# A fused attention and spiking feed-forward block: two normalisations' moments on ScalarE, and a new order of TensorE's instructions around the key projection

## The chip, the cores and the metric

The kernel runs on one core of one Trainium2 chip. The metric is the time of the whole program on the device in microseconds (us), the median of several runs. A core has five engines with queues of their own, each of which works in order: TensorE (PE in the profile; PEld is its weight loads), VectorE (DVE), ScalarE (ACT), GpSimd (POOL) and SyncE (SP, which here only issues DMAs). They meet through semaphores: an instruction waits until a counter has reached a value, and everything behind it on its engine waits with it.

## The reference, cut to what matters

```python
# x: (8, 512, 256) float32; H = 16 heads of dk = 16
x = x + layernorm(attention(layernorm(x)))
x = x + layernorm(feed_forward(layernorm(x)))

def attention(x):
    q, k, v = split(x @ W_qkv.T)              # 16 heads
    k = (k - mean(k)) / sqrt(var(k) + 1e-5)   # over the 16 features of a head
    def step(F, t):                           # over 512 tokens
        F = retention * F + coef * outer(v_t, k_t)
        return F, (W_LTM + F) @ q_t
    return scan(step) @ W_o.T

def feed_forward(x):
    y = square(relu(x @ W_fc.T)) @ W_proj.T   # 256 -> 1024 -> 256
    # 5 steps of a spiking neuron driven by y; the mean of its 5 spikes
    return spikes(y) / 5
```

## The kernel before

A batch is 512 tokens, in four tiles of 128 partitions (TILES). The eight batches go through a software pipeline. Iteration g works on up to four of them at once: the recurrence of batch g ("now"), the output projection and the first half of the feed-forward of batch g-1 ("before", b1), the second half and the spikes of batch g-2 ("two_before", b2), and the input normalisation and first projections of batch g+1 ("after", b). An iteration has 16 slots, and each engine's program is a list of calls under `if s == ...`, so that the order on each engine is written out by hand. Iterations 2 to 6 have all four parts; iteration 1 has no b2, iteration 7 has no batch after.

**The recurrence.** In each slot VectorE does two products (`hebbian`, L953) and two scans over the tokens (`scan`, L963). GpSimd multiplies the states by the queries (`read`, L1237, one instruction a slot), and in every second slot TensorE sums eight such products into PSUM (`sums`, L359). A `read` of slot s waits for the scans of s and, since `prod` has four buffers, for `sums` number s // 2 - 1: `read(g, 14)` waits for `sums(g, 5)`, which is in slot 14 of TensorE. `sums(g, 7)`, in slot 1 of the next iteration, waits for `read(g, 15)`. On GpSimd `add_feed_forward` (L1248) stands between `read(g, 14)` and `read(g, 15)`.

**One bank for many.** The PSUM bank p_a holds in turn the projections of value, key and query (`project`, L311), the variance of the keys (`key_variance`, L332), their spread scales (`key_scale`, L341), the transposed x (`turn_x`, L305) and the transposed x1 (`turn_x1`, L399). Each must have been copied out before the next is written. VectorE's `norm_k` (L945) multiplies the keys by p_a after `key_scale`; for half 0 this is the entry to the recurrence of the next batch. The two banks p_c take the output projection (`project_out`, L372), `down` (L381), `count_spikes` (L389) and `up` (L411) by turns.

**Feed-forward.** `up(b1, 0)` to `up(b1, 7)` stand in slots 10 to 15 of TensorE, and `hidden` on ScalarE follows each: relu out of the bank (L684) and square into `ht` (L686). `hidden(b2, 6)` and `hidden(b2, 7)` are in slot 0 of the next iteration, ahead of `square_k(g, 1)` (L641, L642) in slot 1 and of `copy_y(b1, 1)` in slot 2. `project_out(b1, .)` waits for this last copy (`y_done`). `copy_y` and all the other plain copies have the line of one helper, L628.

**Normalisations.** Norms 1 and 4 get their sums and squares from ScalarE with an accumulator (L600, L609; L715, L726). Norms 2 (of the output projection, `oo`) and 3 (of x1) get theirs from VectorE: four bn_stats (L913) and four bn_aggr (L920), then a square root on ScalarE (`deviation`), a reciprocal on VectorE (`scales`, L926) and four scalings on ScalarE (L617). `low_x` and `low_x1` on GpSimd (L1253) make the low parts that the projections and `up` wait for.

Of the kernel before, what the change touches and what calls it, by code (L numbers as in the profile page):

```python
# [16 lines left out]
P = 128  # L17
KT = D // P
# [50 lines left out]
def build(nc, x, w_qkv, w_o, w_fc, w_proj, w_ltm, head_params, shared_params, ident, head_mask, pick, out):  # L69
    ctx = ExitStack()  # L70
    with ctx:
# [6 lines left out]
        def sem(name):  # L78
# [35 lines left out]
        squares = {n: sb(f"squares{n}", [P, TILES]) for n in (1, 4)}  # L114
# [6 lines left out]
        minus_mean = {n: sb(f"minus_mean{n}", [P, TILES]) for n in (1, 4)}  # L121
# [48 lines left out]
            o_proj o_done n2_stats n2_var n2_dev n2_step n2_done x1_done  # L170
            n3_stats n3_var n3_dev n3_step n3_done  x1_turned x1t_done x1t_high x1t_low
# [124 lines left out]
        def _(pe):  # L296
# [18 lines left out]
            def project_v(b, half):  # L315
                pe.wait_ge(S["xt_low"], at(KT * (b + 1)))
                pe.wait_ge(S["k_done"], at(2 * b + half))
                if half == 0: pe.wait_ge(S["x1t_done"], at(KT * (b - 1)))
                project(b, 2 * D + half * P, "v_proj")
# [65 lines left out]
            def count_spikes(b, pair):  # L385
                pe.wait_ge(S["sign_done"], at(2 * b + pair + 1))
                pe.wait_ge(S["yf_done"], at(TILES * b + 3 + pair))
                for j in range(STEPS):
                    last = pe.matmul(p_c[(pair + 1) % 2][:, :], ident_b[:, :], sign[:, pair, j, :, :],  # L389
                                     start=(j == 0), stop=(j == STEPS - 1))  # L390
                last.then_inc(S["count_done"], 1)

            def turn_x1(b, t):
# [3 lines left out]
                pe.wait_ge(S["x1t_done"], at(KT * b + t))  # L397
                for u in range(TILES):
                    last = pe.transpose(p_a[:, tokens(u)], oo[:, u, t * P:(t + 1) * P], ident_sb[:, :])  # L399
# [65 lines left out]
            def iteration(g, now, before, two_before, after):  # L465
                b, b1, b2 = g + 1, g - 1, g - 2
                for s in range(SLOTS):
# [13 lines left out]
                    if now:  # L481
                        if s == 0: project_v(g, 1)
                        if s == 1: project_k(g, 1)
                        if s == 2: key_variance(g, 1)
# [4 lines left out]
                    if now and s == 5: key_scale(g, 1)  # L489
                    if after and s == 6: turn_x(b, 0)  # L490
                    if two_before and 3 <= s < 7: down(b2, s - 3, before)
                    if after:
                        if s == 7: turn_x(b, 1)
                        if s == 10: project_v(b, 0)
                        if s == 11: project_k(b, 0)
                        if s == 13: project_q(b, 0)
                        if s == 14: key_scale(b, 0)
# [5 lines left out]
                    if after and not before and s == 11: key_variance(b, 0)  # L503
                    if before and after:
                        if s == 10: up(b1, 0)
                        if s == 11:
                            up(b1, 1)
                            key_variance(b, 0)
                            up(b1, 2)
                        if s == 13:  # L510
                            up(b1, 3)
                            up(b1, 4)
                        if s == 14: up(b1, 5)
                        if s == 15:
                            up(b1, 6)
                            up(b1, 7)
# [60 lines left out]
        def _(act):  # L577
# [9 lines left out]
            def deviation(n, b):  # L587
                act.wait_ge(S[f"n{n}_var"], at(b + 1))
                if n in (1, 4):
                    eps = eps_sb[:, 0:1] if n == 1 else eps_sb[:, 2:3] if b == LAST - 1 else eps_sb[:, 1:2]  # L590
                    nc.scalar.activation(dev[n - 1][:, :], squares[n][:, :], ACT.Sqrt, bias=eps, scale=1.0 / D).then_inc(
                        S[f"n{n}_dev"], 1)
                else:
                    nc.scalar.activation(dev[n - 1][:, :], moments[n - 1][:, :, 1], ACT.Sqrt, bias=eps_sb[:, 0:1]).then_inc(
                        S[f"n{n}_dev"], 1)

            def total_x(b):
# [5 lines left out]
                nc.scalar.activation(minus_mean[1][:, :], total[1][:, :], ACT.Identity, scale=-1.0 / D).then_inc(  # L603
                    S["n1_mean"], 1)

            def squares_x(b):
                act.wait_ge(S["n1_mean"], b)
                for u in range(TILES):
                    last = nc.scalar.activation(passed[:, u, :], xa[:, u, :], ACT.Square, bias=minus_mean[1][:, u:u + 1],  # L609
# [65 lines left out]

            def copy_x1t(b, t):
                act.wait_ge(S["x1t_low"], at(KT * (b - 1) + t + 1))
                copy(p_a[:, :], x1f[:, t, :], "x1_turned", KT * b + t + 1, "x1t_done")
# [17 lines left out]
            def signs(b, pair):  # L696
                act.wait_ge(S["yf_done"], at(TILES * b + 2 * (pair + 1)))
                act.wait_ge(S["count_done"], at(2 * (b - 1) + pair + 1))
                for j in range(STEPS):
                    last = nc.scalar.activation(sign[:, pair, j, :, :], yf[:, 2 * pair:2 * pair + 2, :], ACT.Sign,  # L700
                                                bias=drive_sb[:, j:j + 1], scale=BELOW_ONE)
                last.then_inc(S["sign_done"], 1)
# [35 lines left out]
            nc.scalar.activation(dev[0][:, :], moments[0][:, :, 1], ACT.Sqrt, bias=eps_sb[:, 0:1]).then_inc(S["n1_dev"], 1)  # L738
            norm1(0)
# [20 lines left out]
            def iteration(g, now, before, two_before, after):  # L760
                b, b1, b2 = g + 1, g - 1, g - 2
                for s in range(SLOTS):
# [6 lines left out]
                    if s == 0:  # L769
                        if after: total_x(b)  # L770
                        if now: copy_v(g, 1)
                        if two_before:
                            hidden(b2, 6)
                            hidden(b2, 7)
                    if s == 1:
                        if now: square_k(g, 1)
                    if s == 2:
# [5 lines left out]
                    if s == 3:  # L783
# [3 lines left out]
                        if now: copy_q(g, 1)  # L787
                        if after: norm1(b)
                    if s == 4:
                        if before: deviation(2, b1)  # L790
                        if now: spread_k(g, 1)
# [8 lines left out]
                    if s == 7:  # L800
                        if now: copy_key(g)
                        if before: deviation(3, b1)
# [5 lines left out]
                    if s == 9:  # L808
# [5 lines left out]
                        if two_before: signs(b2, 1)  # L814
                        if two_before and after: squares_count(b2, 0)
                    if s == 10:
                        if after: copy_v(b, 0)
                        if two_before and after:
                            total_count(b2, 1)
# [4 lines left out]
                    if s == 11:  # L824
                        if now: copy_y(g, 0)
                        if after: square_k(b, 0)
                        if two_before and after: deviation(4, b2)
                        if before and after: hidden(b1, 0)
                        if after: key_deviation(b, 0)
                        if before and after: hidden(b1, 1)  # L830
# [555 lines left out]
```

## Time and profile before

| | |
|---|---|
| median of 3 runs | 573.79 us (570.6, 573.79, 579.51) |
| the profiled execution: its time, its span | 574.97 us, 573.2 us |
| busy share of the span: PE, PEld, DVE, ACT, POOL | 83%, 55%, 94%, 60%, 67% |
| mean granted clock of TensorE | 0.926 of full speed |
| busy time of VectorE's two large groups, L963 and L953 | 308.8 us and 170.9 us |

The span runs from the first to the last instruction; 1.8 us of the execution's time lie around it. Busy shares are means over stages with different limits, and an engine can be idle for a wait that costs nothing. For a pipeline such as this one the useful question is which chain of waits closes on itself in one iteration.

### The profile page before, as it was taken

The page shows a single profiled execution, that of the slowest core. Times are in us where ns is not written, and L with a number is a line of the kernel's source. Part 1 is how long each engine was busy: PE and PEld are TensorE (multiplying, and loading weights), DVE is VectorE, ACT ScalarE, POOL GpSimd, SP SyncE. Part 2 cuts the span into 40 slices and gives each one's busy share as a digit, 9 for nine tenths or more (in the row PEclk, how much of TensorE's full clock was granted, in tenths as well). Part 3 has the DMA queues.
Part 4 walks back from the last instruction along what each step waited for, and adds up shares of the span by engine and source line. Part 5 has one row for each costly group of instructions (what it writes and reads, how often), then busy time and mean ns, then how long its engine had stood idle before and what let it go on. Part 6 is the DMA issues. An engine that isn't in the chain of part 4 may idle for free.

```text
span 573.2 us, 7812 instructions
## 1 busy us (share of the span) xinstructions
PE 474.5 (83%) x2245; PEld 313.6 (55%) x2252; DVE 539.0 (94%) x858; ACT 341.3 (60%) x788; POOL 386.7 (67%) x206
## 2 busy tenths in 40 slices
PE   4683567549989899979998899989997999897992
PEld 2451234225677466736675557756673667565881
DVE  5699999999999999999999999999999999997767
ACT  5461343444565986687767886697758745763331
POOL 1138996587857968696968794897769686783022
PEclk9698687858989899999999998989999999999997
DMA  7475577556573568647685649455942778410002
GB/s 263 138 196 145 145 186 199 138 154 162 136 206 107 144 168 239 179 116 202 175 211 150 172 122 245 122 152 125 288 135 94 183 215 221 134 39 8 29 2 73
DMA packets 54778, 87.64 MB, mean 153 GB/s; under 512 B 5456, under 2 KB 19408, under 8 KB 54736
## 3 DMA queue, kind: packets, MB, share of 16 engines
q1 hardware_dynamic: 54160, 87.12, 56.2%
q8 instruction: 18, 0.29, 0.2%
q14 instruction: 24, 0.20, 0.1%
q10 hardware_dynamic: 576, 0.03, 0.1%
HBM read 78.74 MB, written 8.39 MB: 152 GB/s over the span
## 4 chain that ended last, share of the span: by engine, by line
PE 54%; DVE 18%; issue 12%; POOL 8%; ACT 6%; DMA 1%; SPq 0%; DVEq 0%; POOLq 0%; ACTq 0%
PE p_c L381 13%; PE p_c L411 11%; DVE state L963 9%; PE p_a L311 7%; PE p_y L359 6%; POOL prod L1237 5%; PE p_c L372 4%; PE p_a L332 2%; PE p_y L350 2%; DVE p_u L953 2%; PE p_a L305 2%; POOL x1t L1253 2%; PE p_u L550 1%; DVE yf L1189 1%; PE p_a L341 1%
## 5 line engine op out<-in xcount | busy, mean ns | idle before, releaser
L1237 POOL TENSOR_TENSOR prod<-state,qf 128x1024 f32<-128x1024 f32 x127 | 300.8, 2375 | 120.3 <-DVE state L963 60.2
L963 DVE TENSOR_TENSOR_SCAN state<-ret,p_u 128x512 f32<-128x512 f32 x256 | 308.8, 1207 | 0.0
L953 DVE TENSOR_TENSOR p_u<-vrep,p_k 128x512 f32<-128x512 f32 x256 | 170.9, 673 | 0.1
L381 PE MATMUL p_c<-wproj_sb,ht 128*128 128x256 f32 x448 | 102.0, 381 | 0.0
L381 PEld LDWEIGHTS p_c<-wproj_sb,ht 128*128 128x128 f32 x448 | 83.5, 190 | 16.8 <-issue 5.0
L311 PE MATMUL p_a<-xt,wqkv_s 128*128 128x512 f32 x276 | 85.1, 448 | 5.7 <-POOL xt L1253 2.1
L411 PE MATMUL p_c<-x1t,wfc_s 128*128 128x512 f32 x324 | 82.7, 401 | 2.3 <-ACT hr L684 1.0
L359 PE MATMUL p_y<-prod,summer 128*32 128x512 f32 x512 | 75.5, 664 | 7.9 <-POOL prod L1237 6.5
L311 PEld LDWEIGHTS p_a<-xt,wqkv_s 128*128 128x128 f32 x276 | 55.2, 210 | 46.0 <-issue 18.7
L411 PEld LDWEIGHTS p_c<-x1t,wfc_s 128*128 128x128 f32 x324 | 59.5, 188 | 18.9 <-POOL x1t L1253 3.4
L700 ACT ACTIVATE sign<-yf,drive_sb 128x512 bf16<-128x512 f32 x60 | 38.1, 710 | 0.2
L684 ACT ACTIVATE hr<-p_c 128x512 f32<-128x512 f32 x56 | 33.2, 593 | 6.5 <-PE p_c L411 5.2
L686 ACT ACTIVATE ht<-hr 128x512 f32<-128x512 f32 x56 | 35.4, 632 | 1.8
L359 PEld LDWEIGHTS p_y<-prod,summer 128*32 128x32 f32 x512 | 10.4, 111 | 37.2 <-issue 25.0
L628 ACT COPY vf<-p_a 128x512 f32<-128x512 f32 x15 | 8.7, 577 | 34.3 <-PE p_a L311 34.3
L372 PE MATMUL p_c<-wo_sb,yt 128*128 128x256 f32 x112 | 28.9, 416 | 0.0
L332 PE MATMUL p_a<-mean_sb,ksq 128*128 128x8 f32 x128 | 17.7, 265 | 13.1 <-ACT ksq L642 13.1
L332 PEld LDWEIGHTS p_a<-mean_sb,ksq 128*128 128x128 f32 x128 | 16.6, 203 | 19.3 <-ACT ksq L642 19.3
L305 PE MATMUL p_a<-ident_sb,xa 128*128 128x128 f32 x64 | 11.9, 317 | 15.8 <-issue 8.0
L372 PEld LDWEIGHTS p_c<-wo_sb,yt 128*128 128x128 f32 x112 | 23.0, 211 | 3.4
L1253 POOL TENSOR_TENSOR xt<-xf,xt 128x512 fp32r<-128x512 f32 x16 | 20.7, 1291 | 5.9 <-ACT xt L628 5.7
L305 PEld LDWEIGHTS p_a<-ident_sb,xa 128*128 128x128 f32 x64 | 8.3, 160 | 25.8 <-issue 14.1
(188 smaller groups left out, 596.4 us busy)
## 6 DMA issues: line engine op xcount, KB each, us to landing
vrep<-v_rows SPq DMA_DIRECT2D x256, 256.0 KB, 4.4
xa<-in_x SPq DMA_DIRECT2D x9, 512.0 KB, 5.0
v_rows<-vf SPq DMA_DIRECT2D x16, 256.0 KB, 2.9
x<-in_x SPq DMA_DIRECT2D x7, 512.0 KB, 6.9
out<-x SPq DMA_DIRECT2D x7, 512.0 KB, 3.3
ht<-in_w_fc SPq DMA_DIRECT2D x1, 1024.0 KB, 7.3
wproj_sb<-in_w_proj SPq DMA_DIRECT2D x1, 1024.0 KB, 10.2
state<-in_w_qkv SPq DMA_DIRECT2D x1, 512.0 KB, 5.9
```

Of the source, the lines that this page charges most:

```text
L311: last = pe.matmul(bank[:, :], wqkv_s[:, i, t, first_col:first_col + P], xt[:, j, t, :], start=(t == i == j == 0), stop=(t == KT - 1 and i ...
L332: last = pe.matmul(p_a[:, u * HH:(u + 1) * HH], ksq[:, u * P:(u + 1) * P], mean_sb[:, :], start=True, stop=True)
L359: last = pe.matmul(p_y[32 * grp:32 * grp + 32, :], summer[:, half, dl, grp, :], prod[:, s % NZ, grp % 2, :], start=False, stop=(dl == 3), ...
L372: last = pe.matmul(p_c[(t + 1) % 2][:, i * D:(i + 1) * D], yt[:, half, tokens(2 * t + i)], wo_sb[:, half, :], start=(half == 0), stop=(hal ...
L381: last = pe.matmul(p_c[(u + 1) % 2][:, 0:D], ht[:, f, tokens(u)], wproj_sb[:, f, :], start=(f == 0), stop=(f == FT - 1))
L411: last = pe.matmul(p_c[(f + 1) % 2][:, :], wfc_s[:, i, t, f * P:(f + 1) * P], x1t[:, j, t, :], start=(t == i == j == 0), stop=(t == KT - 1 ...
L684: nc.scalar.activation(hr[:, f % 2, :], p_c[(f + 1) % 2][:, :], ACT.Relu).then_inc(S["relu_done"], 1)
L686: nc.scalar.activation(ht[:, f, :], hr[:, f % 2, :], ACT.Square).then_inc(S["h_done"], 1)
L700: last = nc.scalar.activation(sign[:, pair, j, :, :], yf[:, 2 * pair:2 * pair + 2, :], ACT.Sign, bias=drive_sb[:, j:j + 1], scale=BELOW_ONE)
L953: v.tensor_tensor(p_u[n % NU][:, :], vrep[:, n % NV, :], p_k[:, :], ALU.mult).then_inc(S["hebb_done"], 1)
L963: v.tensor_tensor_scan(state[:, s % NS, i, :], ret[:, r:r + 1].broadcast_to([P, L]), p_u[n % NU][:, :], 0.0, ALU.mult, ALU.add).then_inc(S ...
L1237: p.tensor_tensor(prod[:, s % NZ, :, :], state[:, s % NS, :, :], qf[:, s // HS, :].unsqueeze(1).broadcast_to([P, 2, L]), ALU.mult).then_in ...
```

## The change

- Norms 2 and 3 lose `statistics` and `moments_of` on VectorE. `squares_o(b1)` in slot 3 of ScalarE squares the four tiles of `oo` with an accumulator (its mean is zero, since W_o is centred), and `squares_x1(b1)` in slot 7 squares the four tiles of x1 with the mean of x as bias. That mean now has to live for three batches, so `minus_mean[1]` becomes three buffers `minus_mean_x`.
- `up(., 7)` goes from slot 15 of TensorE to slot 1 of the next iteration, between `project_k(g, 1)` and `key_variance(g, 1)`; `hidden(b2, 7)` goes behind `square_k(g, 1)`.
- The second half of `turn_x1` goes to the bank p_c[0] and no longer waits for the copy of the first. `count_spikes` of pair 1 then waits for that copy.
- `project_k(b, 0)` follows `project_v(b, 0)` at once in slot 10. For this the five `signs(b2, 1)` on ScalarE are split: two, then `copy_v(b, 0)`, then three, `square_k(b, 0)`, and only then the squares and totals of the counts.
- `key_variance(b, 0)` goes ahead of `up(b1, 1)`, and `key_scale(b, 0)` from slot 14, behind `sums(g, 5)`, to slot 13, ahead of it. `key_scale(g, 1)` goes from slot 5 to slot 4, ahead of a `down`. On ScalarE `norm1(b)` goes behind `spread_k(g, 1)`.

```diff
@@ TensorE
             def project_v(b, half):
-                if half == 0: pe.wait_ge(S["x1t_done"], at(KT * (b - 1)))
+                if half == 0: pe.wait_ge(S["x1t_done"], at(KT * (b - 1) - 1))
...
             def count_spikes(b, pair):
+                if pair == 1: pe.wait_ge(S["x1t_done"], KT * (b + 2))
...
             def turn_x1(b, t):
-                pe.wait_ge(S["x1t_done"], at(KT * b + t))
+                pe.wait_ge(S["x1t_done"], at(KT * (b - 1) + t + 1))
+                if t == 1: pe.wait_ge(S["yf_done"], at(TILES * b))
+                bank = p_a if t == 0 else p_c[0]
...
                         if s == 1: project_k(g, 1)
+                        if s == 1 and two_before: up(b2, 7)
                         if s == 2: key_variance(g, 1)
...
-                    if now and s == 5: key_scale(g, 1)
                     if after and s == 6: turn_x(b, 0)
+                    if now and s == 4: key_scale(g, 1)
...
-                        if s == 10: project_v(b, 0)
-                        if s == 11: project_k(b, 0)
+                        if s == 10:
+                            project_v(b, 0)
+                            project_k(b, 0)
                         if s == 13: project_q(b, 0)
-                        if s == 14: key_scale(b, 0)
...
                         if s == 11:
+                            key_variance(b, 0)
                             up(b1, 1)
-                            key_variance(b, 0)
                             up(b1, 2)
                         if s == 13:
                             up(b1, 3)
                             up(b1, 4)
+                            key_scale(b, 0)
                         if s == 14: up(b1, 5)
-                        if s == 15:
-                            up(b1, 6)
-                            up(b1, 7)
+                        if s == 15: up(b1, 6)
@@ ScalarE
+            def squares_o(b):
+                act.wait_ge(S["o_done"], 2 * (b + 1))
+                for u in range(TILES):
+                    last = nc.scalar.activation(passed[:, u, :], oo[:, u, :], ACT.Square,
+                                                accum_out=squares[2][:, u:u + 1])
+                last.then_inc(S["n2_var"], 1)
+
+            def squares_x1(b):
+                act.wait_ge(S["n1_mean"], b + 1)
+                act.wait_ge(S["x1_done"], b + 1)
+                for u in range(TILES):
+                    last = nc.scalar.activation(passed[:, u, :], x1[b % 2][:, u, :], ACT.Square,
+                                                bias=minus_mean_x[b % 3][:, u:u + 1], accum_out=squares[3][:, u:u + 1])
+                last.then_inc(S["n3_var"], 1)
...
                     if s == 0:
                         if now: copy_v(g, 1)
-                        if two_before:
-                            hidden(b2, 6)
-                            hidden(b2, 7)
+                        if two_before: hidden(b2, 6)
                     if s == 1:
                         if now: square_k(g, 1)
+                        if two_before: hidden(b2, 7)
...
                         if now: copy_q(g, 1)
+                        if before:
+                            squares_o(b1)
+                            deviation(2, b1)
+                    if s == 4:
+                        if now: spread_k(g, 1)
                         if after: norm1(b)
-                    if s == 4:
-                        if before: deviation(2, b1)
-                        if now: spread_k(g, 1)
...
                         if now: copy_key(g)
-                        if before: deviation(3, b1)
+                        if before:
+                            squares_x1(b1)
+                            deviation(3, b1)
...
-                        if two_before: signs(b2, 1)
-                        if two_before and after: squares_count(b2, 0)
+                        if two_before and after: signs(b2, 1, 0, 2)
+                        if two_before and not after: signs(b2, 1)
                     if s == 10:
                         if after: copy_v(b, 0)
+                        if two_before and after: signs(b2, 1, 2, 3)
+                        if after: square_k(b, 0)
                         if two_before and after:
+                            squares_count(b2, 0)
                             total_count(b2, 1)
                             squares_count(b2, 1)
...
                         if now: copy_y(g, 0)
-                        if after: square_k(b, 0)
                         if two_before and after: deviation(4, b2)
-                        if before and after: hidden(b1, 0)
                         if after: key_deviation(b, 0)
-                        if before and after: hidden(b1, 1)
+                        if before and after:
+                            hidden(b1, 0)
+                            hidden(b1, 1)
@@ VectorE
-                    if before and s == 4:
-                        statistics(2, b1, oo, "o_done", 2 * (b1 + 1))
-                        moments_of(2, b1)
...
-                    if before and s == 7:
-                        statistics(3, b1, x1[b1 % 2], "x1_done", b1 + 1)
-                        moments_of(3, b1)
```

## Rows read from the trace of the kernel before

**Rows 1.** The page, parts 1 and 4: busy time, and the chain that ended last.
```profile
PE 474.5 (83%) x2245; PEld 313.6 (55%) x2252; DVE 539.0 (94%) x858; ACT 341.3 (60%) x788; POOL 386.7 (67%) x206
...
PE 54%; DVE 18%; issue 12%; POOL 8%; ACT 6%; DMA 1%; SPq 0%; DVEq 0%; POOLq 0%; ACTq 0%
```

**Rows 2.** Timeline of VectorE, start, duration, [idle before]: norm_k at an iteration's end.
```profile
88.72 0.67 DVE L945 TENSOR_TENSOR p_k<-p_a,kc 128x512 f32<-128x512 f32 x1
...
149.41 0.70 DVE L945 TENSOR_TENSOR p_k<-p_a,kc 128x512 f32<-128x512 f32 x1 [0.69 <-PE p_a L341]
...
211.73 0.70 DVE L945 TENSOR_TENSOR p_k<-p_a,kc 128x512 f32<-128x512 f32 x1 [0.88 <-PE p_a L341]
...
272.73 0.70 DVE L945 TENSOR_TENSOR p_k<-p_a,kc 128x512 f32<-128x512 f32 x1 [0.68 <-PE p_a L341]
...
457.03 0.70 DVE L945 TENSOR_TENSOR p_k<-p_a,kc 128x512 f32<-128x512 f32 x1 [0.68 <-PE p_a L341]
```

**Rows 3.** Who TensorE waited for, iteration 4 (272.7 to 333.7): us, times, longest.
```profile
PE p_c L389 <- ACT sign L700: 1.8, 1, 1.8
PE p_a L332 <- ACT ksq L642: 1.4, 1, 1.4
PE p_a L399 <- ACT oo L617: 1.1, 1, 1.1
PE p_a L399 <- ACT x1f L628: 0.9, 1, 0.9
```

**Rows 4.** Timeline of VectorE in iteration 4: the moments of norm 3.
```profile
303.57 1.38 DVE L913 BATCH_NORM_STATS2 stats<-x 128x6 f32<-128x256 f32 x4
304.98 0.38 DVE L920 BATCH_NORM_AGGREGATE moments<-stats 128x2 f32<-128x6 f32 x4
```

**Rows 5.** Groups by line: one square with an accumulator over 128x256.
```profile
L609 ACT ACTIVATE passed<-xa,minus_mean 128x256 f32<-128x256 f32 x28 | 13.8, 496 | 0.0
```

**Rows 6.** Timeline of GpSimd in slot 9 of iteration 4: the last low part of x.
```profile
312.94 1.28 POOL L1253 TENSOR_TENSOR xt<-xf,xt 128x512 fp32r<-128x512 f32 x1
```

**Rows 7.** Timeline of TensorE: project_k(b, 0) right behind project_v(b, 0), in iteration 0.
```profile
72.00 2.93 PE L311 MATMUL p_a<-xt,wqkv_s 128*128 128x512 f32 x6 [0.73 <-ACT vf L628]
```

**Rows 8.** Timeline of ScalarE in slot 11 of iteration 4: the copy in square_k(b, 0).
```profile
322.18 0.59 ACT L641 COPY kc<-p_a 128x512 f32<-128x512 f32 x1 [0.41 <-PE p_a L311]
```

**Rows 9.** Timeline of TensorE from the end of iteration 3 into iteration 4.
```profile
271.05 1.07 PE L359 MATMUL p_y<-prod,summer 128*32 128x512 f32 x8
272.04 0.66 PE L341 MATMUL p_a<-ident_sb,krx 128*128 128x128 f32 x4
272.45 4.45 PE L411 MATMUL p_c<-x1t,wfc_s 128*128 128x512 f32 x18
...
279.46 1.06 PE L359 MATMUL p_y<-prod,summer 128*32 128x512 f32 x8
...
284.43 3.70 PE L372 MATMUL p_c<-wo_sb,yt 128*128 128x256 f32 x16
```

**Rows 10.** Timeline of GpSimd in the same stretch: read 14, add_feed_forward, reads 15 and 0.
```profile
272.29 2.41 POOL L1237 TENSOR_TENSOR prod<-state,qf 128x1024 f32<-128x1024 f32 x1 [0.48 <-PE p_y L359]
274.66 2.40 POOL L1248 TENSOR_TENSOR x<-x,spk 128x1024 f32<-128x1024 f32 x1
277.02 4.75 POOL L1237 TENSOR_TENSOR prod<-state,qf 128x1024 f32<-128x1024 f32 x2
```

**Rows 11.** Timeline of ScalarE in the same stretch: hidden(b2, 7), then copy_y.
```profile
281.24 0.58 ACT L684 ACTIVATE hr<-p_c 128x512 f32<-128x512 f32 x1
281.86 0.63 ACT L686 ACTIVATE ht<-hr 128x512 f32<-128x512 f32 x1
...
283.35 0.59 ACT L628 COPY yt<-p_y 128x512 f32<-128x512 f32 x1
```

**Rows 12.** project_out's matmuls in two stretches of iteration 2: us, PE busy, PEld busy, PEclk, DMA share, GB/s.
```profile
160.90:164.30 3.40, 3.03 (x7) 2.56 (x8) 0.50 1.05 268
161.20:166.50 5.30, 5.21 (x16) 4.09 (x16) 0.70 1.05 263
```

## What the change should do to the time

> **What bounds the kernel now.** I read the page first: VectorE is busy 94% of the span, yet the chain that ended last runs 54% on TensorE and 18% on VectorE [rows 1]. So the fullest engine isn't plainly the limit. The timeline of VectorE settles the size of an iteration by `norm_k`, its last step: 60.7 us for iteration 1 (88.72 to 149.41), 62.3 us for iteration 2, 61.0 us for iteration 3, and 307.6 us for iterations 2 to 6 together (149.41 to 457.03), that is three of 61.0 and two of 62.3 [rows 2]. At each of these entries but the first VectorE stands idle for 0.7 to 0.9 us until TensorE's `key_scale` is there [rows 2]. VectorE is thus nearly full, but it is TensorE that lets it in.
>
> The next view is who TensorE waited for: in iteration 4 it waits four times, 1.8, 1.4, 1.1 and 0.9 us, 5.2 us in all, always for ScalarE and never for VectorE [rows 3]. TensorE's own loop, about 55.8 us of work and 5.2 us of round trips, makes the 61.0 us. The change takes work from VectorE and goes for three of those four waits. What counts is whether the loop of TensorE gets shorter.
>
> **VectorE's part.** Four bn_stats and four bn_aggr take 303.57 to 305.28, 1.7 us [rows 4]; norms 2 and 3 have a set each, so 3.4 us leave VectorE in each of iterations 1 to 7. Where TensorE sets the pace these 3.4 us become idle time in front of `norm_k` or of a reciprocal. Where VectorE does, they come off the time. ScalarE gets twice 4 x 0.496 = 2.0 us [rows 5]. In slot 7 these come in place of a wait for the moments, which ended at 305.36 [rows 4]: from the copies ahead of it on ScalarE I work out 305.3 for the new squares too, so nothing is gained or lost on x's way to its low part and on to `project_v(b, 0)`. Bounds for each set: 0 and its own 2.0 us late.
>
> **Two banks.** `turn_x1(., 1)` waits 0.9 us for the copy of the first half [rows 3], and no longer will. But `project_v(b, 0)` also needs the last low part of x, which GpSimd makes from 312.94 to 314.22 [rows 6], just when TensorE comes by today. The chain to it (`sums(g, 1)`, three reads, two low parts) doesn't change. I take 0; the other end is 0.9 us an iteration. The Trainium skill ("Perfetto Trace Analysis", Optimizing Tensor Performance, Matmuls) advises rotating independent matmul groups through different banks, so that one is copied out under the next. By that rule the 0.9 us would be won; the low part's row speaks against it here.
>
> **Key projection at once, variance one tile ahead.** Behind `project_v` TensorE will wait 0.7 us for the copy of the values, as in iteration 0 [rows 7], in place of the 1.8 us for the signs [rows 3]. But `up(b1, 2)` still needs ScalarE's first relu, and ScalarE has the same list to do before it, only in another order. It loses one idle 0.41 us [rows 8], gains 0.2 us of waiting for the end of `project_v`, and the second bank has spared it 0.2. I take 0.3 us earlier for `project_q(b, 0)`; bounds 0 and 1.1 (1.8 - 0.7). `key_scale(b, 0)` ahead of `sums(g, 5)` then costs its 0.4 us (272.04 to 272.45 [rows 9]) on the way to `sums(g, 5)`, which so comes 0.1 us later than today.
>
> **The last up tile.** It is moved into the 1.4 us in which TensorE waits for the squares of the keys before `key_variance(g, 1)` [rows 3]. What it leaves behind is the question. Today `sums(g, 5)` starts at 271.05 and `sums(g, 7)` at 279.46 [rows 9]. Between them GpSimd does read 14 (which waits for `sums(g, 5)`), add_feed_forward and read 15: 272.29 to 279.4, with no gap [rows 10]. So `sums(g, 7)` starts the moment read 15 is done, and TensorE is there at that moment too, because it had `key_scale`, three up tiles, `sums(g, 6)` and `project_v` to do. Take out `key_scale` (0.4) and one up tile (1.45, a third of the 4.4 us of the three in L411's row [rows 9]) and TensorE is there 1.8 us early and waits. The 1.4 us filled are given back in front of `sums(g, 7)`. Gain 0.
>
> And there is a new wait. `hidden(b2, 7)` now stands ahead of `copy_y(b1, 1)` on ScalarE and cannot start before `up(b2, 7)` is done; behind `copy_y` stands TensorE's `project_out(b1, 0)`. From the start of `sums(g, 7)` to `project_out` it is 279.46 to 284.43, 4.97 us [rows 9]. After: the sums 1.0, `project_k` 1.5 (six matmuls of 512 columns like an up tile), the up tile 1.5 and about 0.15 to the end of its last matmul, 0.1 to ScalarE, relu and square until the next instruction starts 1.17 (0.62 + 0.55), `copy_y` 0.59, 0.05 back to TensorE [rows 9, 11]: 6.06 us (I put the two hand-overs at 0.1 and 0.05 as an estimate). That is 1.1 us more in each iteration with b2. TensorE would wait about 1 us at L372.
>
> **The sum.** The period of iterations 2 to 6: 61.0 + 0.1 + 1.1 = 62.2 us, five times +1.2 = +6.0. Iteration 1 has no b2, so neither `up(b2, 7)`, hidden(b2, 7) nor add_feed_forward. TensorE is idle there while VectorE sets the pace: of the 3.4 us I take 2.9, since a wait of ScalarE's new squares for x1 gives some back (bounds 2 and 3.4). Iteration 7 again waits for TensorE at the start, and later VectorE must wait at norm 3 for x1: 0.3 gained, bounds 0 and 3.4. Iteration 0 and the tail: 0. Sum: +6.0 - 2.9 - 0.3 = +2.8 us.
>
> **The clock.** Iteration 2, of 62.3 us, has its `project_out` in 5.21 instead of 3.70 us [rows 9, 12], at a granted clock of 0.50 of full speed (1.2 GHz) in the stretch after 160.90; just before it TensorE waits for the squares of the keys and does the small matmuls of the variance, as it does in every iteration [rows 3]. Only iteration 2's is in the rows; I put the second iteration of 62.3 us down to the same, and keep these 2 x 1.3 us as they are: TensorE's idle time in an iteration goes from 5.2 to about 6.5 us, but is spread out.
>
> So 573.2 + 2.8 = 576.0 us of span, and 577.8 for that execution with its 1.8 us around the span. The median shown is 1.2 us under the profiled execution: 576.6 us.
>
> **Rivals.**
> *Faster, VectorE is the bound.* If the 3.4 us come off every iteration from 1 to 7, 24 us go: 550 us. For it: the 94%. Against it: the 0.7 us at each `norm_k`, which then would have to go as well. It holds if TensorE's loop falls to 57.6 us, so all four waits must go. Chance 0.05. The Trainium skill ("Perfetto Trace Analysis", Identifying the Most-Contended Engine) would have one look at the engine with the highest occupancy, here VectorE, and shorten it first, with this result.
> *Faster, the waits simply go.* If GpSimd's read 15 is done when TensorE comes to `sums(g, 7)`, the 1.4 us are kept, and the change of order at the value projection gives 1.0: a period of 58.6 us, 5 x 2.4 = 12 us, with the 3 us of iterations 1 and 7 and the 2.6 us of slow clock also gone: 556 us. It decides at read 15: it would have to end 1.8 us sooner, for which read 14 would have to start before `sums(g, 5)` ends. Chance 0.11.
> *Same, only one of my two waits.* Without the wait of `project_out`: 5.5 us less than my sum, 571 us. Or with the wait at `project_out` but the up tile's gain kept: 570 us. Chance 0.24.
> *Slower by the clock.* More short waits next to short matmuls could bring the lower clock in every iteration, behind the variance and behind the transposes. A slow `project_out` costs 1.5 us, a slow projection behind the transposes about as much by the same doubling of six matmuls' 1.4 us: 3.0 us in five iterations instead of the 2.6 now is +12.4: 589 us. From two further slow stretches an iteration on it decides. Chance 0.10. The Trainium skill ("TensorE: Matmul & The Clock Gate", A second HAM failure mode) tells of frequent micro-idles between matmul groups that make the clock swing between its two levels; by that the whole loop would be in this case.
> *My sum:* chance 0.50, with 572 to 582 us as its own range.
>
> **Numbers.** The range of 8 in 10 leaves out the two faster rivals (0.16) and the far end of the slower one: 563 to 587 us. A change of under 2% (11.5 us) is about what a measurement of this kernel can't tell from none. Faster by more, under 562.3 us: 0.16. Slower by more, over 585.3: 0.10. Within: 0.74.
>
> **What would show it.** In the profile after: VectorE's busy time down by 24 us to about 515, and its waits for the reciprocals (L926) and `norm_k` up by as much. A wait of TensorE at L359 for GpSimd's prod of 1.8 us in each of iterations 3 to 6; one at L372 for ScalarE's yt of 1 us; one at the second L311 of slot 10 for vf of 0.7 us; none at L332. `norm_k` to `norm_k` 62.2 us. If L359 shows no such wait and the period is under 60, the sum is wrong at read 15. If L372 doesn't wait, it is wrong at `copy_y`. If VectorE has no more idle time than now, the first rival is right.

## The result, and the profile after

| | before | after |
|---|---|---|
| median of 20 runs | 574.22 us | 577.12 us |
| the profiled execution: its time, its span | 574.97 us, 573.2 us | 580.05 us, 578.2 us |
| busy share: PE, PEld, DVE, ACT, POOL | 83, 55, 94, 60, 67% | 83, 55, 89, 63, 67% |
| mean granted clock of TensorE | 0.926 | 0.921 |

The ratio is 1.0046, with a 95% interval of 1.0024 to 1.0068: a little slower, and under 2%. The forecast median was 576.6 us. The profiled execution of the changed kernel took 2.9 us more than the median, so an average execution may have fewer of the slow stretches that its trace shows below. VectorE has 24.5 us less to do [rows 1] and the kernel gains nothing by it. The page after, busy time:

```profile
PE 478.6 (83%) x2245; PEld 319.3 (55%) x2252; DVE 514.5 (89%) x746; ACT 365.2 (63%) x901; POOL 385.6 (67%) x206
```

The timeline of VectorE after, `norm_k` for half 0 (L969 now; start, duration), for rows 2:

```profile
87.04 0.67 DVE L969 TENSOR_TENSOR p_k<-p_a,kc 128x512 f32<-128x512 f32 x1
...
144.50 0.67 DVE L969 TENSOR_TENSOR p_k<-p_a,kc 128x512 f32<-128x512 f32 x1
...
205.00 0.68 DVE L969 TENSOR_TENSOR p_k<-p_a,kc 128x512 f32<-128x512 f32 x1
...
270.05 0.68 DVE L969 TENSOR_TENSOR p_k<-p_a,kc 128x512 f32<-128x512 f32 x1
...
335.11 0.67 DVE L969 TENSOR_TENSOR p_k<-p_a,kc 128x512 f32<-128x512 f32 x1
...
396.93 0.67 DVE L969 TENSOR_TENSOR p_k<-p_a,kc 128x512 f32<-128x512 f32 x1
...
458.77 0.67 DVE L969 TENSOR_TENSOR p_k<-p_a,kc 128x512 f32<-128x512 f32 x1
```

Iteration 1 now takes 57.5 us (60.7 before). Iterations 2 to 6 take 60.5, 65.1, 65.1, 61.8 and 61.8, together 314.3 us against 307.6 [rows 2]. Iteration 0 is 1.7 us shorter, and from the last of these lines to the end it is 119.4 us against 116.2. The sum, -1.7 - 3.2 + 6.7 + 3.2, is the 5.0 us between the two spans.

Who TensorE waited for after, in iteration 5 (333 to 395 us; us in total, times, longest), for rows 3. The lines are `sums` (L360), `turn_x1` (L403), `project_out` (L373), `project` (L312) and `up` (L415):

```profile
PE p_y L360 <- POOL prod L1255: 1.8, 1, 1.8
PE p_a L403 <- ACT oo L618: 1.1, 1, 1.1
PE p_c L373 <- ACT yt L629: 1.1, 1, 1.1
PE p_a L312 <- POOL xt L1271: 0.9, 1, 0.9
PE p_a L312 <- ACT vf L629: 0.7, 1, 0.7
PE p_c L415 <- ACT hr L700: 0.5, 1, 0.5
```

Two more, of 0.2 us each, are left out. Of the four waits of before one is still there (L403, 1.1 us). The three that went, 4.1 us, have become five that come to 5.0. Two of these decide, and the timelines of TensorE, ScalarE and GpSimd after show them at the start of iteration 5 (`norm_k` at 335.11), for rows 9, 11 and 10:

```profile
338.67 1.06 PE L360 MATMUL p_y<-prod,summer 128*32 128x512 f32 x8
339.67 1.66 PE L312 MATMUL p_a<-xt,wqkv_s 128*128 128x512 f32 x6
343.10 1.07 PE L360 MATMUL p_y<-prod,summer 128*32 128x512 f32 x8 [1.77 <-POOL prod L1255]
344.10 1.66 PE L312 MATMUL p_a<-xt,wqkv_s 128*128 128x512 f32 x6
345.59 1.54 PE L415 MATMUL p_c<-x1t,wfc_s 128*128 128x512 f32 x6
346.97 1.02 PE L333 MATMUL p_a<-mean_sb,ksq 128*128 128x8 f32 x8
349.05 3.69 PE L373 MATMUL p_c<-wo_sb,yt 128*128 128x256 f32 x16 [1.05 <-ACT yt L629]
```

```profile
347.17 0.60 ACT L700 ACTIVATE hr<-p_c 128x512 f32<-128x512 f32 x1 [0.29 <-PE p_c L415]
347.80 0.63 ACT L702 ACTIVATE ht<-hr 128x512 f32<-128x512 f32 x1
348.33 0.57 ACT L629 COPY yt<-p_y 128x512 f32<-128x512 f32 x1
```

```profile
335.96 2.43 POOL L1255 TENSOR_TENSOR prod<-state,qf 128x1024 f32<-128x1024 f32 x1 [0.84 <-PE p_y L360]
338.32 2.41 POOL L1266 TENSOR_TENSOR x<-x,spk 128x1024 f32<-128x1024 f32 x1
340.67 4.71 POOL L1255 TENSOR_TENSOR prod<-state,qf 128x1024 f32<-128x1024 f32 x2
```

`key_variance` (L333) follows the moved up tile without a gap, so the wait it was moved into is gone. But TensorE stands for 1.77 us in front of `sums(g, 7)` until read 15 is done (the first of the two in GpSimd's last line, half of 4.71 us, so at about 343.0), and for 1.05 us more in front of `project_out`, because ScalarE takes relu and square of this very up tile before it copies `yt`.

And where VectorE's time went, its longest waits after, over the whole span (us, times, longest):

```profile
DVE rdev L950 <- ACT dev L595: 39.2, 13, 4.8
...
DVE p_k L969 <- PE p_a L342: 1.0, 1, 1.0
```

It now stands in front of the reciprocals, for ScalarE's square roots. Before, it waited at `norm_k` (5.5 us in seven waits over the whole span).

### The profile page after: what moved, and what is told of

Same layout as the page of the kernel before. It is cut to its first block, busy times and chain, and to the rows that moved or that the text cites. A ratio compares the mean times of both kernels' runs of the same rounds, so it can differ in the third digit from the quotient of the medians.

```text
span 578.2 us, 7797 instructions
## 1 busy us (share of the span) xinstructions
PE 478.6 (83%) x2245; PEld 319.3 (55%) x2252; DVE 514.5 (89%) x746; ACT 365.2 (63%) x901; POOL 385.6 (67%) x206
## 4 chain that ended last, share of the span: by engine, by line
PE 54%; DVE 17%; issue 10%; POOL 9%; ACT 8%; DMA 1%; SPq 0%; DVEq 0%; POOLq 0%; ACTq 0%
PE p_c L382 15%; DVE state L987 11%; PE p_c L415 10%; PE p_y L360 8%; PE p_a L312 7%; POOL prod L1255 6%; PE p_c L373 5%; DVE p_u L977 2%; PE p_y L351 2%; ACT sign L716 2%; PE p_a L306 2%; POOL xt L1271 2%; ACT passed L742 1%; PE p_u L555 1%; PE p_a L342 1%
## 5 line engine op out<-in xcount | busy, mean ns | idle before, releaser
L382 PE MATMUL p_c<-wproj_sb,ht 128*128 128x256 f32 x448 | 100.4, 379 | 0.0
L312 PE MATMUL p_a<-xt,wqkv_s 128*128 128x512 f32 x276 | 83.5, 441 | 11.9 <-POOL xt L1271 6.3
L415 PE MATMUL p_c<-x1t,wfc_s 128*128 128x512 f32 x324 | 84.3, 404 | 4.4 <-ACT hr L700 3.6
L360 PE MATMUL p_y<-prod,summer 128*32 128x512 f32 x512 | 73.1, 645 | 17.2 <-POOL prod L1255 15.7
L312 PEld LDWEIGHTS p_a<-xt,wqkv_s 128*128 128x128 f32 x276 | 52.8, 202 | 51.9 <-issue 17.8
L415 PEld LDWEIGHTS p_c<-x1t,wfc_s 128*128 128x128 f32 x324 | 60.3, 191 | 25.9 <-issue 11.9
L950 DVE RECIPROCAL rdev<-dev 128x4 f32<-128x4 f32 x29 | 4.8, 166 | 39.6 <-ACT dev L595 39.2
L373 PE MATMUL p_c<-wo_sb,yt 128*128 128x256 f32 x112 | 34.3, 475 | 6.5 <-ACT yt L629 6.5
L360 PEld LDWEIGHTS p_y<-prod,summer 128*32 128x32 f32 x512 | 10.4, 111 | 46.9 <-issue 26.0
L373 PEld LDWEIGHTS p_c<-wo_sb,yt 128*128 128x128 f32 x112 | 26.6, 242 | 11.9 <-issue 6.8
L642 ACT COPY kc<-p_a 128x512 f32<-128x512 f32 x16 | 9.3, 583 | 30.5 <-PE p_a L312 30.5
L629 ACT COPY yf<-p_c 128x256 f32<-128x256 f32 x28 | 10.1, 361 | 28.1 <-PE p_c L382 28.1
L629 ACT COPY qf<-p_a 128x512 f32<-128x512 f32 x15 | 8.8, 586 | 23.9 <-PE p_a L312 23.9
```

The lines of the kernel that those rows point to most:

```text
L312: last = pe.matmul(bank[:, :], wqkv_s[:, i, t, first_col:first_col + P], xt[:, j, t, :], start=(t == i == j == 0), stop=(t == KT - 1 and i ...
L360: last = pe.matmul(p_y[32 * grp:32 * grp + 32, :], summer[:, half, dl, grp, :], prod[:, s % NZ, grp % 2, :], start=False, stop=(dl == 3), ...
L373: last = pe.matmul(p_c[(t + 1) % 2][:, i * D:(i + 1) * D], yt[:, half, tokens(2 * t + i)], wo_sb[:, half, :], start=(half == 0), stop=(hal ...
L382: last = pe.matmul(p_c[(u + 1) % 2][:, 0:D], ht[:, f, tokens(u)], wproj_sb[:, f, :], start=(f == 0), stop=(f == FT - 1))
L415: last = pe.matmul(p_c[(f + 1) % 2][:, :], wfc_s[:, i, t, f * P:(f + 1) * P], x1t[:, j, t, :], start=(t == i == j == 0), stop=(t == KT - 1 ...
```

## The experiments

The ratio is that of each kernel's runs to the runs of the kernel before on the same chip. The period is `norm_k` to `norm_k` in iterations 3 to 6 at full clock, from the trace. The median of the kernel before was 573.6 to 575.3 us from one set of runs to the other, so a difference between medians of two sets is uncertain by 1 to 2 us, and the ratios are the better measure there.

| | median | ratio to before (95%) | period |
|---|---|---|---|
| the change | 577.1 us | 1.0046 (1.0024 to 1.0068) | 61.8 us |
| copy_y first | 563.8 us | 0.981 (0.978 to 0.984) | 60.6 us |
| up 7 back | 567.1 us | 0.987 (0.984 to 0.990) | 60.6 us |
| read 15 first | 568.2 us | 0.987 (0.982 to 0.991) | 61.6 us, never at full clock |
| both edits | 553.8 us | 0.963 (0.961 to 0.966) | 58.8 us |
| both, low part earlier | 554.9 us | 0.966 (0.964 to 0.969) | 58.3 us |
| both, moments on VectorE | 568.2 us | 0.990 (0.988 to 0.992) | 60.1 us |
| moments alone, on before | 572.9 us | 0.998 (0.996 to 1.000) | 60.6 us |
| two banks alone, on before | 576.0 us | 1.003 (1.001 to 1.006) | 61.0 us |
| read 15 first, on before | 575.1 us | 1.001 (0.998 to 1.004) | 61.0 us |
| the change, wait filled | 571.1 us | 0.996 (0.992 to 0.999) | 61.8 us |

### copy_y first: the wait at project_out

```diff
                     if s == 1:
                         if now: square_k(g, 1)
-                        if two_before: hidden(b2, 7)
                     if s == 2:
                         if before: copy_y(b1, 1)
+                        if two_before: hidden(b2, 7)
```

> The changed kernel with copy_y(b1, 1) back ahead of hidden(b2, 7) on ScalarE; nothing else. My theory: TensorE's wait for yt in front of project_out (1.1 us in each of iterations 2 to 7) is on the loop, so about 6 us go: 571 us, norm_k to norm_k 60.7 us in an iteration at full clock. Rival: the wait only takes up slack that GpSimd or VectorE would take otherwise: 577 us and 61.8 us as in the changed kernel.

Two lines exchanged, and 13.4 us less than with the change. The timeline of TensorE of this run, the same place in the iteration:

```profile
330.03 1.07 PE L360 MATMUL p_y<-prod,summer 128*32 128x512 f32 x8 [1.78 <-POOL prod L1255]
...
333.90 1.02 PE L333 MATMUL p_a<-mean_sb,ksq 128*128 128x8 f32 x8
334.78 3.70 PE L373 MATMUL p_c<-wo_sb,yt 128*128 128x256 f32 x16
```

`project_out` now follows the variance at once. The wait in front of the sums is as long as ever. The period falls by 1.2 us, as expected; the 7 us that this makes in six iterations are half of what was measured. The other half is put down to the clock: no iteration from 2 to 6 of this trace is slower than 60.65 us, and the granted clock is 1.00 in each, where the changed kernel has two iterations of 65.1 and four with a `project_out` of 5.38 us (iterations 2, 3, 4 and 7). The mechanism was right and the size was half of the truth.

### up 7 back: what the move of the tile is worth

```diff
-                        if s == 1 and two_before: up(b2, 7)
...
-                        if s == 15: up(b1, 6)
+                        if s == 15:
+                            up(b1, 6)
+                            up(b1, 7)
```

with `hidden(b2, 7)` back in slot 0 of ScalarE.

> The changed kernel with up(., 7) back in slot 15 and hidden(., 7) back in slot 0. My theory: sums(g, 7) starts when read 15 ends either way. The wait of 1.8 us at the sums shrinks to about 0.3, the wait of 1.2 us for the squares of the keys is back, and the wait for yt is gone: 571 us, like the run with copy_y first. Rival, that filling the wait in front of key_variance is worth its 1.4 us and only copy_y's place spoils it: undoing both gives 1.1 back and loses 1.4 in five iterations, 578 to 579 us.

The waits of TensorE in its iteration 5 (330 to 392 us):

```profile
PE p_a L333 <- ACT ksq L644: 1.2, 1, 1.2
...
PE p_y L360 <- POOL prod L1256: 0.4, 1, 0.4
```

The 1.2 us for the squares of the keys are back, and those for read 15 are down from 1.8 to 0.4. The period is 60.6 us, the same as with the tile moved and `copy_y` first. So moving the tile gains nothing as long as read 15 holds the sums: it only says where TensorE waits. Iteration 2 is the check: there no add_feed_forward stands ahead of read 15 and TensorE doesn't wait at L360 in either run, and with the tile moved (copy_y first) it takes 57.6 us, with the tile back 59.2, both at full clock. So the fill is worth 1.6 us where read 15 doesn't hold the sums. This run measured 3.4 us longer than copy_y first; besides iteration 2, its trace has two iterations of 62.3 us, with a stretch at the lower clock.

### read 15 first, and both edits

```diff
                     if s == 0 and before: read(b1, SLOTS - 1)
+                    if s == 0 and before and g >= 3: add_feed_forward(g - 3)
...
-                    if two_before and after and s == 15: add_feed_forward(b2)
```

and `store_out`, which waits for the result, in slot 3 and no longer in slot 2.

> The changed kernel with add_feed_forward moved on GpSimd from ahead of read 15 to behind it (slot 0 of the next iteration), and the store that waits for it one slot later. My theory: sums(g, 7) waits 1.8 us for read 15 only because of these 2.4 us; without them the wait goes and the loop is 1.8 us shorter in iterations 3 to 7: 568 us, period 60.0 us. Rival: something else holds the loop (VectorE, ScalarE): 577 us.

The median is as expected, 568.2 us, but the period is not. The wait at L360 is gone, and the 1.1 us at L373 are left. Here is `project_out` in this run, and the stretch in which it ran (us, then busy time of PE, PEld, DVE, ACT, POOL with counts, the granted clock, DMA share, GB/s):

```profile
340.05 5.38 PE L373 MATMUL p_c<-wo_sb,yt 128*128 128x256 f32 x16 [1.05 <-ACT yt L629]
```

```profile
339.90:343.30 3.40, 3.25 (x8) 2.66 (x9) 3.30 (x6) 2.45 (x11) 3.06 (x2) 0.56 1.06 283
```

5.38 us and not 3.7, at a granted clock of 0.56 on the mean of the stretch: behind the wait the clock was at the lower level, 1.2 GHz, and in this trace so in each of iterations 2 to 6, at the same place. 61.6 less these 1.7 us is the 60.0 us expected.

> The changed kernel with both edits: copy_y first and read 15 ahead of add_feed_forward. My theory: the two add up, period 61.8 - 1.1 - 1.8 = 58.9 us, 15 us less: 562 us. VectorE's own work, about 57.5 us an iteration, is not reached yet. Rival: each hides behind the other or a third wait (the squares of the keys, ScalarE's relu) takes their place: 568 us.

Both edits together give 553.8 us and a period of 58.8 us, against 58.9 expected. The whole is 8 us shorter than expected. The clock accounts for it: in this trace no iteration from 2 to 6 takes over 58.8 us, and the granted clock is 1.00 in each. Its row on the page, 40 slices of the span in tenths of full speed:

```profile
PEclk9786558958999999999999999999999999999997
```

And the timeline of TensorE, with neither wait:

```profile
323.60 1.66 PE L312 MATMUL p_a<-xt,wqkv_s 128*128 128x512 f32 x6
325.19 1.07 PE L360 MATMUL p_y<-prod,summer 128*32 128x512 f32 x8
326.19 1.65 PE L312 MATMUL p_a<-xt,wqkv_s 128*128 128x512 f32 x6
327.68 1.54 PE L415 MATMUL p_c<-x1t,wfc_s 128*128 128x512 f32 x6
329.06 1.02 PE L333 MATMUL p_a<-mean_sb,ksq 128*128 128x8 f32 x8
329.94 3.70 PE L373 MATMUL p_c<-wo_sb,yt 128*128 128x256 f32 x16
```

This is the best version: 3.7% less than the kernel before, 4.0% less than the changed one by their medians.

### The parts of the change alone

**Moments alone**: the kernel before, with only the moments of norms 2 and 3 moved to ScalarE, in their old slots.

> The kernel before with one part of the change: the moments of norms 2 and 3 by ScalarE, in the same slots. My theory: the loop of iterations 2 to 6 stays at 61.0 us, VectorE is idle 3.4 us more in each, and only iteration 1 gets about 3 us shorter: 571 us. Rival, that VectorE at 94% is the bound: 3.4 us in each of seven iterations, 550 us.

572.9 us. The period goes from 61.0 to 60.6 us, so 0.4 us an iteration were to be had, not 0 and not 3.4. VectorE, with 3.4 us less to do, is busy 57.10 us of 60.60 in iteration 5 and waits for the rest, 1.0 us of it in front of `norm_k` at full clock (0.7 before; 1.67 in the first line, at the end of an iteration of 62.1 us) and 1.5 us in front of a reciprocal, where it did not wait before. Its timeline in this run:

```profile
331.18 0.70 DVE L963 TENSOR_TENSOR p_k<-p_a,kc 128x512 f32<-128x512 f32 x1 [1.67 <-PE p_a L342]
...
364.06 0.18 DVE L944 RECIPROCAL rdev<-dev 128x4 f32<-128x4 f32 x1 [1.50 <-ACT dev L591]
```

The first rival, that VectorE sets the pace at 94%, falls with this run. ScalarE's new squares don't hide a gain either: TensorE's four waits of rows 3 are there with the same lengths to 0.1 us. Iteration 1 became 1.9 us shorter, where about 3 were expected.

**Two banks alone**: the kernel before, with only the second half of `turn_x1` in p_c[0].

> The kernel before with one part of the change: the second half of turn_x1 in its own bank. My theory: the wait of 0.9 us in front of the second transposes goes and comes back in front of project_v(b, 0), which needs the last low part of x from GpSimd: 574 us, no change. Rival, the rule that such a rotation wins the wait: 0.9 us in six iterations, 569 us.

576.0 us, a little slower rather than faster, and the period stays at 61.0 us. From the waits of TensorE around iteration 5 of this run:

```profile
PE p_a L311 <- POOL xt L1256: 1.1, 1, 1.1
```

The 0.9 us for the copy [rows 3] are gone and stand again, as 1.1 us, in front of `project_v`, which waits for the low part of x. The small loss isn't settled: in this trace iterations 1, 2, 4 and 6 have a stretch at the lower level (iteration 1 takes 63.4 us), in that of the kernel before iterations 1, 2 and 5.

**Read 15 first, on the kernel before.**

> The kernel before with read 15 ahead of add_feed_forward, and nothing of the change. My theory: in the kernel before TensorE comes to the sums just when read 15 is done, so ending it 2.4 us earlier is worth at most some tenths: 574 us, period 61.0 us. Rival: read 15 holds the loop already before the change: 1 to 2 us in five iterations, 565 to 569 us.

575.1 us, period 61.0 us. The same edit that takes 9 us from the changed kernel takes nothing from the one before. Read 15 becomes a wait only once the up tile and `key_scale` have left the stretch in front of the sums.

### With both edits: the next limits

> The run with both edits, but with the moments of norms 2 and 3 back on VectorE. My theory: with TensorE's loop at 58.9 us, VectorE's 57.5 + 3.4 = 60.9 us become the bound: 571 to 573 us. Rival: VectorE still has slack, and the time stays at that of both edits, 562 us.

568.2 us, 14.4 more than with the moments on ScalarE. In the changed order the 3.4 us on VectorE do count: in iteration 4 of this run VectorE is busy 59.93 of 60.00 us and waits for nobody. (`deviation(2, b1)` stays in slot 3 of ScalarE and there waits for VectorE's moments, but no wait comes back to VectorE from it.) The moments are worth 0.4 us an iteration in the kernel before, and 1.3 us once TensorE's loop is shorter than VectorE's work. It is somewhat faster than expected: 60.1 us where I had put 60.9, from a floor of 57.5 that was 0.7 too high. In both edits alone VectorE is busy 56.99 of 59.0 us:

```profile
330.00:389.00 59.00, 55.58 (x285) 37.66 (x285) 56.99 (x73) 49.01 (x127) 47.73 (x24) 1.00 0.66 179
```

> The run with both edits, and the last low part of x one slot earlier on GpSimd, ahead of read 8. My theory: the wait of 0.9 us in front of project_v(b, 0) goes, and with two banks nothing else stands there; up(b1, 2) still needs the first relu, so 0.5 to 0.9 us in five iterations: 3 us less than both edits alone, 559 us. VectorE's floor of 57.5 us comes near. Rival: ScalarE's list up to the first relu is the bound there: no change to both edits alone.

```diff
-                    if after and s in (7, 9): low_x(b, (s - 7) // 2)
+                    if after and s in (7, 8): low_x(b, s - 7)
```

The wait for the low part goes, and the next wait of TensorE, for `vf`, grows from 0.7 to 1.3 us: ScalarE is not done with the transposes and the first two signs. The period is 58.3 us, 0.4 less, of the 0.5 to 0.9 expected. The median is no lower. In the profiled execution of this run iteration 0 took 61.9 us instead of 59.3, for a reason told below, which hides a gain of this size. The edit moves the low part in iteration 0 too, so that this loss may be its own.

### The clock: the wait filled

```diff
                 pe.wait_ge(S["relu_done"], at(FT * b - 1 + t))
+                if b >= 1 and t == 0:
+                    for i in range(2):
+                        pe.matmul(p_c[1][:, 0:D], wo_sb[:, 0, 0:P], wo_sb[:, 0, :], start=True, stop=True)
                 pe.wait_ge(S["y_done"], at(2 * (b + 1)))
```

> The changed kernel with two extra matmuls (0.84 us together at full clock, their output is overwritten) in TensorE's wait for yt in front of project_out. The wait itself, its place and the order on ScalarE stay. My theory: the granted clock falls behind this wait because TensorE does next to nothing there but the eight small matmuls of the variance; with work in it the clock stays up, the period stays at 61.8 us and the two iterations of 65 us go: 570 to 572 us. Rival: it is the wait of 1.8 us in front of the sums, two stages earlier, that brings the clock down: 577 us as in the changed kernel.

571.1 us, by work that nobody needs (the two matmuls are four instructions in the trace): 6.0 us less than the change by the medians, 5.2 by the ratios. The period stays at 61.8 us:

```profile
335.44 1.06 PE L360 MATMUL p_y<-prod,summer 128*32 128x512 f32 x8 [1.77 <-POOL prod L1258]
...
340.18 1.11 PE L372 MATMUL p_c<-wo_sb 128*128 128x256 f32 x4
341.28 3.72 PE L376 MATMUL p_c<-wo_sb,yt 128*128 128x256 f32 x16
```

`project_out` starts where it did, but at full clock, in 3.72 us in every iteration from 2 to 7. One iteration of 63.3 us is left, whose slow stretch comes right behind the wait for the sums. So the lower clock can come behind that wait as well; in this trace it does so once.

## Why the prediction was right, point by point

**The bound.** That TensorE's loop sets the pace and VectorE only fills it is shown by moments alone (0.4 us an iteration of the 3.4) and by VectorE's 39.2 us in front of the reciprocals.

**Two banks: 0.** Shown by two banks alone. After the change the wait is there as predicted, 0.9 us at L312 for `xt`.

**The up tile: 0, for read 15.** The wait is 1.8 us as worked out, in iterations 3 to 6. In iteration 2 it isn't there, and the 0 was wrong: the sum has its +1.2 for five iterations, though the wait was named for 3 to 6 only. Shown from both sides: the tile back gives the same period as `copy_y` first, and the wait goes when read 15 does, which takes nothing from the kernel before.

**The wait at project_out: +1.1 us.** Shown by copy_y first, at 1.2 us. From `sums(g, 7)` to `project_out` it is now 343.10 to 349.05, 5.95 us, where the prediction had 6.06.

**Key projection and key_scale.** Mis-sized: this part was to cost 0.1 us and gives 0.1. From the start of `project_out` to that of the next `sums(g, 5)` it is 47.5 us (349.05 to 396.54, below) against 47.6 before. `project_q(b, 0)` came 0.5 us sooner rather than 0.3 (42.7 us behind `project_out`, 43.2 before), and pays for `key_scale` with it.

```profile
396.54 1.06 PE L360 MATMUL p_y<-prod,summer 128*32 128x512 f32 x8
```

The rest of the loop, to the next `project_out`, was to cost 1.1 and costs 1.0 us (396.54 to 410.89, 14.35 us, against 271.05 to 284.43, 13.38 [rows 9]). So the period at full clock is 61.8 us and not 62.2.

**Iteration 1: -2.9.** It was -3.2, within its bounds. **Iteration 7: -0.3.** It is +3.2 from `norm_k` to the end. Of this 2.2 us are only a shift of the mark: `norm_k` comes earlier against TensorE, 13.9 us before `project_out` (458.77 to 472.67) and not 11.7 (457.03 to 468.72). From this `project_out` on it is 1.0 us more, and that one ran at the lower clock, in 5.38 us, which is 1.7 of it: without the clock this end would be 0.7 us shorter, where I had 0.3.

**The clock: as before.** This is the term that failed. I kept 2 x 1.3 us, on the ground that the waits are spread out. In the profiled execution iteration 2 has a slow `project_out`, 1.7 us too long:

```profile
155.43 5.38 PE L373 MATMUL p_c<-wo_sb,yt 128*128 128x256 f32 x16 [1.05 <-ACT yt L629]
```

And two iterations take 65.1 us, 3.2 over the last two, each with two stretches at the lower level. The windows view of iteration 3 (columns as above):

```profile
211.10:214.50 3.40, 1.62 (x11) 0.61 (x11) 3.40 (x5) 1.71 (x3) 3.40 (x2) 0.97 0.89 263
214.50:217.90 3.40, 3.40 (x10) 2.65 (x9) 3.40 (x5) 1.08 (x2) 3.25 (x3) 0.53 0.98 240
217.90:221.40 3.50, 2.38 (x15) 2.06 (x15) 1.45 (x2) 2.76 (x8) 2.19 (x1) 0.96 1.08 300
221.40:224.80 3.40, 3.40 (x10) 2.75 (x9) 1.95 (x4) 1.97 (x8) 0.00 (x0) 0.54 1.09 277
```

TensorE is busy for 1.62 us in the first of them (the wait for the sums) and 2.38 in the third (the variance and the wait for `yt`), and behind each the clock is at about half. In all that is 8.1 us (1.7 and twice 3.2) in iterations 2 to 6 against 2.6 in the kernel before, 5.5 more.

So the sum (576.0 us of span, 578.2 measured) came out close by luck, through misses that nearly cancel. Too low were the clock, by these 5.5 us, and iteration 7, by 3.5. Too high were the loop at full clock by 0.4 us in each of iterations 3 to 6, iteration 2 by 3.4 (58.8 us at full clock and not 62.2: 1.8 for the wait that isn't there, about 1.2 for `norm_k`, which after iteration 1 still comes later against TensorE), iteration 1 by 0.3, and iteration 0 by 1.7, for which I had nothing. Why iterations 2 to 4 have slow stretches and iterations 5 and 6, with the same waits as 3 and 4, have none isn't settled by these runs.

The slower rival had the right mechanism and too high a share: it needed two more slow stretches in every iteration, and the trace has six in all in iterations 2 to 7. The faster rival was right on the point that decides it, though not for this change: with read 15 ahead and `copy_y` first the period is 58.8 us, where it had put 58.6.

## What to carry to other kernels

Before a step is moved into an idle gap, ask what its old place covered. In iterations 3 to 6 GpSimd's chain from `sums(g, 5)` to `sums(g, 7)` ran exactly as long as TensorE's work between the two, and the gap reopened in front of the sums. Follow the step's consumer too: on an in-order engine a relu placed ahead of a copy makes everybody who needs the copy wait for the tile. An engine that is 94% busy may still be led by another; relieving it pays only when the other loop is shortened too, as the moments show (0.4 us an iteration before, 1.3 after).

## What the runs showed of the hardware

A short wait costs TensorE more than its length. 1.1 us in front of `project_out` cost the wait itself and, at times, 1.7 us more of `project_out` at 1.2 GHz (5.38 against 3.69 us for the same sixteen instructions). Two matmuls of no use in that gap won 5 to 6 us. The Trainium skill ("TensorE: Matmul & The Clock Gate", A second HAM failure mode) describes frequent micro-idles between groups of matmuls that make the clock swing between its two levels. The trace agrees in this, with a granted clock of 0.97, 0.53, 0.96 and 0.54 in four successive stretches of iteration 3.

A small operation of VectorE can last until a running one of GpSimd's ends. In iteration 0 of the kernel before, the scaling of `osum`, two numbers a partition, took 1.91 us and ended when GpSimd's product did:

```profile
79.30 2.39 POOL L1237 TENSOR_TENSOR prod<-state,qf 128x1024 f32<-128x1024 f32 x1 [0.33 <-DVE state L963]
...
79.80 1.91 DVE L931 TENSOR_SCALAR osum<-osum 128x2 f32<-128x2 f32 x1
```

In the changed kernel's trace GpSimd was idle at that moment, and the same operation took 0.17 us:

```profile
79.86 0.17 DVE L955 TENSOR_SCALAR osum<-osum 128x2 f32<-128x2 f32 x1
```

This is the 1.7 us that iteration 0 won, and not by the change: of the twelve kernels' traces ten have iteration 0 at 59.3 us, two of them (two banks alone and read 15 first, on the kernel before) with VectorE's and GpSimd's programs of that iteration as before. In the run with the low part earlier the operation took 2.75 us, to the end of the second of two GpSimd operations in a row. The Trainium skill ("Perfetto Trace Analysis", Optimizing Scalar/DVE Operations) says that the two engines share an SBUF read port, which an operation of VectorE with two ports locks for itself. The rows fit that, with VectorE as the one who waits for the lock; no run here took the operation apart.
